# Two matmuls of 256 columns for each one of 512 in stage one of a two-stage mixture-of-experts kernel, and another filling of the opening

## The reference, cut to what matters

```python
# stage one, per token's expert e (chosen by its id)
h   = layernorm(x)
g   = silu(h @ ctx[e].T);  u = h @ ctx[e].T
x1  = x + (g * u) @ ctx[e].T        # einsum('bsf,df->bsd')
# stage two, per token's expert e = argmax(router_w @ layernorm(x1))
g, u = bitlinear(h2, wg[e]), bitlinear(h2, wu[e])
out  = x1 + bitlinear(square(relu(g)) * u, wd[e])
```

## Time and profile before

| | us |
|---|---|
| two timed runs | 252.14, 252.72 (median 252.43) |
| profiled execution | 252.44 |
| its span | 250.5 |
| PE busy (matmuls) | 230.1, 92% of the span |
| PEld busy (weight loads) | 168.0, 67% |
| DVE busy | 216.7, 87% |
| ACT busy | 208.7, 83% |
| POOL busy | 166.1, 66% |

### The profile page before, as it was taken

How to read it: one execution, slowest core, us unless ns; L and a number is a source line. 1 busy time by engine, 2 the same in 40 slices (tenths; PEclk the granted TensorE clock), 3 DMA queues, 4 the chain that set the end, 5 groups by cost and what they waited for, 6 DMA issues and landing times.

```text
span 250.5 us, 5540 instructions
## 1 busy us (share of the span) xinstructions
PE 230.1 (92%) x1319; PEld 168.0 (67%) x1327; DVE 216.7 (87%) x675; ACT 208.7 (83%) x324; POOL 166.1 (66%) x325
## 2 busy tenths in 40 slices
PE   2398999999999999999999999999989999999980
PEld 2245788888888888888888888887335445454430
DVE  5979999989898888898889888969999999999881
ACT  2767799799889888898889878888889999999970
POOL 4362675868778777778777745345737788686863
PEclk9999999999999999999999999999999999999997
DMA  5999953946753589885764545534358982212110
GB/s 194 425 357 361 429 210 107 377 154 238 252 184 102 193 306 404 285 311 207 252 218 139 176 185 213 174 98 152 99 149 258 303 294 93 99 69 79 66 42 0
DMA packets 13725, 51.70 MB, mean 206 GB/s; under 512 B 2750, under 2 KB 2750, under 8 KB 10112
## 3 DMA queue, kind: packets, MB, share of 16 engines
q1 hardware_dynamic: 8816, 37.91, 43.0%
q0 software_dynamic: 4880, 13.44, 14.6%
HBM read 40.49 MB, written 13.48 MB: 215 GB/s over the span
## 4 chain that ended last, share of the span: by engine, by line
PE 76%; DVE 11%; DMA 5%; ACT 3%; issue 3%; POOL 0%; SPq 0%; DVEq 0%; ACTq 0%
PE bank L1576 35%; PE bank L1698 22%; PE bank L1560 9%; PE bank L1668 5%; DMA ternary<-weight_chunks 3%; PE bank L1690 2%; PE bank L1802 2%; DVE ctx_lo L1007 1%; DMA staged<-x_rows 1%; PE bank L1595 1%; DVE ternary L964 1%; ACT ternary L705 1%; DVE p L1101 1%; DMA token_ids<-token_ids_in 1%; DVE ternary L1026 1%
## 5 line engine op out<-in xcount | busy, mean ns | idle before, releaser
L1698 PE MATMUL bank<-ternary,qT 128*128 x178 | 45.1, 379 | 0.5
L705 ACT ACTIVATE ternary<-staged 128x2048 bf16<-128x2048 f32 x20 | 38.0, 1900 | 2.0 <-DMA staged<-weight_chunks 2.0
L711 ACT ACTIVATE ternary<-staged,w_scale 128x1536 int16<-128x1536 f32 x20 | 31.4, 1576 | 2.3 <-DVE w_scale L1021 0.6
L571 POOL DMA_INDIRECT x_rows<-row,store_at x19 | 25.5, 1343 | 6.8 <-POOL store_at L563 5.0
L1698 PEld LDWEIGHTS bank<-ternary,qT 128*128 128x128 bf16 x184 | 17.2, 98 | 16.3 <-issue 1.0
L482 POOL DMA_INDIRECT x<-x_rows,gather x16 | 18.5, 1155 | 10.3 <-DVE gather L976 6.5
L652 POOL DMA_INDIRECT out_rows<-late_rows,late_token x18 | 19.6, 1089 | 7.9 <-DVE late_rows L1366 5.5
L1698 PE MATMUL bank<-ternary,rT 128*128 x90 | 23.4, 379 | 1.4 <-ACT rT L809 0.8
L758 ACT ACTIVATE p<-bank,rstd 128x512 f32<-128x512 f32 x19 | 13.0, 686 | 12.6 <-PE bank L1576 12.6
L1101 DVE SCALAR_TENSOR_TENSOR p<-bank,rstd,p 128x512 f32<-128x512 f32 x19 | 14.2, 749 | 9.6 <-ACT p L758 9.6
L1576 PE MATMUL bank<-ctx_hi,pT_hi 128*128 x76 | 22.3, 415 | 0.1
(11 more groups left out here) (237 smaller groups left out, 650.9 us busy)
## 6 DMA issues: line engine op xcount, KB each, us to landing
staged<-weight_chunks SPq DMA_DIRECT2D x20, 1024.0 KB, 5.4
late_rows<-x_rows SPq DMA_DIRECT2D x18, 260.0 KB, 3.7
ternary<-ctx_chunks SPq DMA_DIRECT2D x4, 1024.0 KB, 8.3
ternary<-weight_chunks SPq DMA_DIRECT2D x4, 1024.0 KB, 9.4
x_rows<-filler SPq DMA_DIRECT2D x1, 2080.0 KB, 12.6
staged<-x_rows SPq DMA_DIRECT2D x5, 260.0 KB, 2.9
x_rows<-row,store_at POOLq DMA_INDIRECT x19, 6.2
out_rows<-late_rows,late_token POOLq DMA_INDIRECT x18, 2.8
```

Source lines behind the costliest of these rows:

```text
L571: pool.indirect_dma_start(x1_rows, bass.IndirectOffsetOnAxis(ap=store_at[b % ROWS][:, :], axis=0), row[b % ROWS][:, :], None, bounds_check ...
L705: nc.scalar.activation(ternary[:, m * K * D:(m + 1) * K * D], staged_of(i), ACT.Abs, accum_out=abs_sum[:, 2 * i:2 * i + 1]).then_inc(abs_r ...
L711: nc.scalar.activation(ternary[:, m * K * D + DVE_COLS:(m + 1) * K * D].bitcast(I16), staged_of(i)[:, DVE_COLS:], ACT.Copy, scale=w_scale[ ...
L1698: last = pe.matmul(ps[:, :], side(left[:, :], k), ternary[:, bass.ds(e * (3 * K * D) + (kind * K + k) * D, D)], start=(k == 0), stop=(k == ...
```

## The change

Each matmul of a product of stage one is issued twice, for columns 0 to 255 and for 256 to 511, with the same stationary operand; only the very first of a product carries the start flag. In the opening, five instead of nine fill matmuls are issued ahead of the first transposes, and then `fill_groups(3)`: 12 float32 matmuls with 32 stationary columns and 128 moving ones, whose outputs go in turn to partitions 0, 32, 64 and 96 of bank 3, and so to four groups of columns of the array. It waits for `made` to reach 8, which `ident` does. Everything on the other engines stays.

```diff
-WARM_UP = (9, 3)
+WARM_UP = (5, 3)
...
                     for k in range(K):
-                        last = pe.matmul(ps[:, :], left[:, k * P:(k + 1) * P],
-                                         right[:, bass.ds(e * (K * D) + k * D, D)],
-                                         start=(n == 0 and k == 0), stop=(n == 2 and k == K - 1))
+                        for half in range(2):
+                            cols = slice(half * D // 2, (half + 1) * D // 2)
+                            last = pe.matmul(ps[:, cols], left[:, k * P:(k + 1) * P],
+                                             right[:, bass.ds(e * (K * D) + k * D + half * D // 2, D // 2)],
+                                             start=(n == 0 and k == 0 and half == 0), stop=(n == 2 and k == K - 1),
+                                             skip_group_check=True)
                 return last
...
+            def fill_groups(n):
+
+                pe.wait_ge(made, 8)
+                for i in range(n):
+                    for g in range(K):
+                        pe.matmul(bank[3][32 * g:32 * (g + 1), 0:P], before[:, 0:32], ident[:, :],
+                                  start=(i == 0), stop=(i == n - 1))
+
...
             load_expert(0)
             warm_up(WARM_UP[0])
+            fill_groups(3)
             transpose_h(0)
```

## The result

The changed kernel takes **255.89 us** (255.84 and 255.95), against 252.43 before: 3.46 us more, a ratio of 1.0137 with a 95% interval of 1.0086 to 1.0188. It is slower, but by less than 2%. Its profiled execution took 255.84 us, its span 253.8.

A forecast was written before the change was run, and what follows sets the result against it. TensorE was taken to bound stage one, busy 136.90 of 137.00 us. 252.44 + 6.5 (halves in 38 products) - 0.15 (shorter wait) + 0.25 (opening) = 259.0 us; range 250.7 to 261.5.

The forecast's parts named there:

- the likeliest case: Stage one's float32r matmuls: a fixed 14 ns each, 259.0 us in all, own range 257 to 260.5; chance 0.55.
- the first two rivals: Stage one: surcharge goes with the columns, 253.5 us, chance 0.16; weight loads set the pace, 250.9 us, chance 0.13.
- a smaller surcharge: Stage one's float32r matmuls: 11 instead of 14 ns each, bringing the time below 257.5 us; chance 0.11.
- the price per product: Each stage-one product takes 2.90 instead of 2.73 us: 12 x 0.0142 = 0.170 us more.
- the count of products: Stage one: all 38 products' added time reaches the end, 6.5 us, less 0.15 us for a wait.
- the opening: Before the first transposes: 24 fill passes at the queue's pace take 1.9 us, ending late by 0.25 us.
- A price per matmul: Stage one: a fixed 14 ns per float32r matmul, so one of 256 columns starts every 0.1209 us.
- columns alone: Stage one: surcharge goes with the columns, a half every 0.114 to 0.117 us, 253.5 us in all; chance 0.16.
- the loads alone: Stage one: weight loads set the pace, a half every 0.112 us, 250.9 us in all; chance 0.13.
- The queue: Stage one: added issue costs nothing under two microseconds of lead; rival, lead lost: about 268 us, chance 0.05.
- The wait at 51.9: Second product at 51.9 us waits for a weight transfer, 3.02 against 2.87 us; later TensorE waits less, -0.15 us.

The follow-up runs named there:

- Uneven sizes: The changed kernel with a product's three terms split 256+256, 320+192 and 384+128 columns instead of equal halves: 265.2 us.
- Stage two: Against the kernel before: small fills as in the change, stage one's products whole, stage two's bfloat16 products halved with a register instruction ahead of each half: 280.89 us.

## Why the prediction was right or wrong

The range of 250.7 to 261.5 holds 255.89, and the sign and its cause are right. The number, 259.0, is 3.1 us too high, and outside the 257 to 260.5 that I gave the likeliest case. The largest chance, 0.60, stood on slower by over 2%; what happened lies in the 0.37 by size. Of the mechanisms behind that number it is neither of the first two rivals but the rest of the forecast's own case, a smaller surcharge, to which I gave 0.11. Two terms of the sum were too large, the price per product (1.9 us) and the count of products (0.8 us, against 0.15 allowed for), and the opening was put 0.5 us too high for this execution.

**A price per matmul** on top of the columns held. The forecast distance was 0.1209 us; it is 0.120 in two terms and 0.118 in the first. By columns alone it would be 0.114 to 0.117, by the loads alone 0.112. Uneven sizes show the floor of about 0.11 us but don't tell a fixed price from one that goes with the columns. What makes the price isn't shown, nor that it is the same 14 ns at every size: an added matmul cost 0.127 / 12 and 0.115 / 12, about 10 ns.

**Its size per product was too large, and this is the larger error:** 0.170 forecast, 0.12 measured (0.13 and 0.11). I took one distance for all twelve matmuls. In the first term, behind the wait for the first load, the 512-column matmuls start 0.232, 0.231 and 0.227 us apart and not 0.2275, and the halves 0.118 and not 0.1209, so this third of the product pays 0.02 to 0.03 us instead of the 0.057 forecast; the other two pay 0.04 to 0.05 each. That made 38 x 0.05 = 1.9 us of the error.

**The count was wrong too, and here it was the reasoning that failed:** "whatever a product gains or loses is gained or lost ... once for each of the 38 products, less the few places where TensorE waits", with 0.15 us for those places. I inferred from 136.90 busy us in 137.00 that there is no slack from 28 us on. But a matmul's record lasts 0.39 us where the next starts after 0.23, so waits of up to 0.16 us ahead of a group leave no idle time on PE. Iterations of 8.10 and 8.24 us in the early blocks beside 7.98 later would have shown them, and so would the chain, which in that trace isn't on TensorE up to 51.9 us. About 0.8 of the first ten products' 1.2 us was absorbed: shown by the halves in early blocks alone. That 28 x 0.12 = 3.4 is the measured whole is partly luck: some 0.4 us of the early products did reach the end, and an opening that was 0.24 us ahead took most of it back.

**The opening:** the price of 24 passes was 1.9 us against 1.28 measured, since four groups do run side by side; 0.25 forecast, nothing measurable in times. The Trainium skill's rule (TensorEngine Tiling (Array Packing), Key Properties) that different tiles load and multiply in parallel agrees with the traces: six fours of passes, each in 0.214 us, on four groups; one pass in each 0.213 us on one, at the same lower clock. I had put it beside the sum when it should have been in it.

**The queue** was rightly costed at nothing in stage one. It begins the product of 72.41 at 70.7 and ends the register load by about 73.5, while the product runs to 75.4:

```profile
L1578 PEldq FUSED_REGOPS  x8: 46/46/46, 70.7 to 71.7; - x8
...
L1588 PEldq TENSOR_LOAD <-expert x1: 307/307/307, 73.2 to 73.2; - x1
```

The lead shrank from 2.0 to 1.7 us. Stage two shows what happens when it is gone, so the rival was real, only not here.

**The wait at 51.9** gave back what I said (3.02 us against 2.87 before, 2.99 like the other second products after); the rest was absorbed in the blocks ahead of it.

## What to carry to other kernels

Read the price of a matmul from the distance between starts, for each size and each place in the group, and split it into columns, what comes on top, and a floor: here 11 to 13 ns on top for a float32r half of 256 columns, and no less than about 0.11 us for a matmul with its load. Where large and small matmuls alternate, read the sum of a pair. A full busy row of TensorE does not prove that it never waits; compare the lengths of like iterations, look whether the chain that ended last is on TensorE there, and count only the iterations that are at the floor. Before cutting matmuls smaller, add up what the queue issues per matmul, registers included, since a queue without a lead costs far more than its own pace.

## What the runs showed of the hardware that I had not expected

- The moment at which TensorE comes to the higher clock moves from execution to execution with the same instructions ahead of it. By the distances between starts, one profiled execution of the changed kernel was there by 16.5 us (the four transposes of h in 0.50 us), the other only by 17.41 (0.78 us for the transposes, then three wide fills 0.215 apart). The kernel with swapped terms, whose opening is the same, came to it at 21.9, though its h came 0.5 us later too. That execution ended 1.9 us later than the changed kernel's, more than any choice of fills gave.
- Whatever term stands first in a product, its halves go at 0.118 us and not 0.120, while whole matmuls go slower there (up to 0.232, not 0.227). The cause stays open.
- Float32 matmuls with 32 stationary columns and 128 moving ones: on four groups of columns four passes went in each 0.214 us, on one group a single pass in 0.213 us at the lower clock and in 0.109 at the higher. So twelve such matmuls took 1.28 us on four groups and 3.98 on one.
